# Post-norm attention and mixture of experts on one core: the gate and up products wait by PSUM bank, and the last expert's normalisation is shared out differently

## The reference

```
x = layernorm(x + attn(x))                       # 4 x 2048 tokens of 256 channels, no softmax: causal sigmoid
logits = x @ w_router; top1 of 32 experts; gate = probability of the chosen one
buf[e] = the first C = 320 tokens of expert e
g = buf[e] @ w_gate[e];  u = buf[e] @ w_up[e]     # 320 x 256 by 256 x 256
y = (silu(g) * u) @ w_down[e]
x = layernorm(x + gate * y)                       # (x - mean) / sqrt(var + 1e-5)
```

## Time and profile before

| | |
|---|---|
| time, median of 3 runs | 561.07 us (560.72 to 561.43) |
| profiled execution: its time, its span | 560.36 us, 558.6 us |
| PE, PEld busy in the span | 524.0 us (94%), 458.0 us (82%) |
| DVE, ACT, POOL busy in the span | 407.4 us (73%), 378.3 us (68%), 363.1 us (65%) |
| TensorE clock granted, mean | 0.99 |

### The profile page before, as it was taken

The page is one execution under the profiler, slowest core; times in us unless marked ns, Lnnn a source line. Parts: engine busy times, 40 slices in busy tenths (PEclk is TensorE's granted clock), DMA queues, the critical chain, the costliest instruction groups (busy, mean ns, idle before and its releaser), DMA issues.

```text
span 558.6 us, 12192 instructions
## 1 busy us (share of the span) xinstructions
PE 524.0 (94%) x4028; PEld 458.0 (82%) x4028; DVE 407.4 (73%) x1025; ACT 378.3 (68%) x776; POOL 363.1 (65%) x496
## 2 busy tenths in 40 slices
PE   6999999999999999999999899999999999999970
PEld 5889888898988888888989458888888888888860
DVE  3785868866868856779585637887888888888870
ACT  5886968859778788788686215666666666666641
POOL 4647878787867778786772541566666666666672
PEclk9999999999999999999999999999999999999995
DMA  7994232244332532336901052666666677673200
GB/s 251 375 355 149 76 95 64 93 149 97 115 73 77 165 95 89 61 128 178 341 28 59 21 155 37 201 195 208 201 208 211 191 213 221 207 239 85 60 34 35
DMA packets 91903, 81.54 MB, mean 146 GB/s; under 512 B 31626, under 2 KB 83066, under 8 KB 91840
## 3 DMA queue, kind: packets, MB, share of 16 engines
q1 hardware_dynamic: 84848, 66.39, 40.6%
q0 software_dynamic: 6912, 14.30, 7.3%
q10 hardware_dynamic: 80, 0.07, 0.0%
HBM read 44.33 MB, written 37.90 MB: 147 GB/s over the span
## 4 chain that ended last, share of the span: by engine, by line
PE 75%; DVE 11%; issue 5%; ACT 3%; POOL 3%; DMA 1%; DVEq 0%; POOLq 0%; ACTq 0%; SPq 0%
PE ps L910 11%; PE ps L911 11%; PE ps L912 11%; PE ps L886 10%; PE ps L1063 6%; PE ps L1071 5%; PE ps L1064 5%; DVE v_hl L1265 4%; PE ps L1097 3%; PE ps L1039 3%; PE ps L929 2%; ACT hl_ring L796 2%; DVE hl_ring L1354 2%; PE ps L1089 2%; PE ps L942 1%
## 5 line engine op out<-in xcount | busy, mean ns | idle before, releaser
L910 PE MATMUL ps<-v_hl,hl_ring 128*128 128x256 f32 x544 | 176.0, 323 | 0.4 <-DVE hl_ring L1159 0.3
L911 PE MATMUL ps<-v_hl,hl_ring 128*128 128x256 f32 x544 | 153.4, 282 | 0.0
L912 PE MATMUL ps<-v_hl,hl_ring 128*128 128x256 f32 x544 | 153.1, 281 | 0.0
L910 PEld LDWEIGHTS ps<-v_hl,hl_ring 128*128 128x128 f32 x544 | 103.3, 190 | 15.7 <-issue 1.4
L1159 DVE TENSOR_TENSOR hl_ring<-ps,hl_ring 128x512 fp32r<-128x512 f32 (+3 forms) x160 | 93.2, 601 | 18.0 <-ACT ps L687 14.2
L911 PEld LDWEIGHTS ps<-v_hl,hl_ring 128*128 128x128 f32 x544 | 103.5, 190 | 2.4
L912 PEld LDWEIGHTS ps<-v_hl,hl_ring 128*128 128x128 f32 x544 | 103.2, 190 | 0.0
L685 ACT ACTIVATE hl_ring<-ps 128x512 fp32r<-128x512 f32 (+3 forms) x160 | 85.9, 537 | 23.6 <-PE ps L886 10.5
L886 PE MATMUL ps<-q_t,k_t 128*128 128x512 bf16 (+3 forms) x320 | 85.4, 350 | 2.8 <-ACT k_t L766 1.1
L1063 PE MATMUL ps<-hl_ring,v_hl 128*128 128x320 f32 x256 | 82.0, 332 | 6.2 <-DVE act_r L1373 5.8
L687 ACT ACTIVATE ps<-ps 128x512 f32<-128x512 f32 (+3 forms) x160 | 86.9, 543 | 0.0
(11 more groups left out here) (161 smaller groups left out, 1090.7 us busy)
## 6 DMA issues: line engine op xcount, KB each, us to landing
expert_rows<-xs SPq DMA_DIRECT2D x40, 258.0 KB, 5.6
xs<-expert_rows SPq DMA_DIRECT2D x32, 258.0 KB, 2.9
xall<-in_L_attn_x_dram SPq DMA_DIRECT2D x16, 512.0 KB, 4.4
out_dram<-alone SPq DMA_DIRECT2D x16, 512.0 KB
xall<-in_L_ffn_w_gate_dram SPq DMA_DIRECT2D x32, 256.0 KB, 4.4
xall<-in_L_ffn_w_up_dram SPq DMA_DIRECT2D x32, 256.0 KB, 4.7
xall<-in_L_ffn_w_down_dram SPq DMA_DIRECT2D x32, 256.0 KB, 5.0
xs<-expert_rows SPq DMA_DIRECT2D x31, 64.5 KB
```

Source lines behind the costliest of these rows:

```text
L910: mm(o, ah, v_hl[:, 0, j, :], start=(j == 0 and i % 2 == 0), stop=False, skip_group_check=True)
L911: mm(o, ah, v_hl[:, 1, j, :], start=False, stop=False, skip_group_check=True)
L912: last = mm(o, al, v_hl[:, 0, j, :], start=False, stop=(j == GT * g + i), skip_group_check=True)
```

## The change

1. In `gate_up`, gate's products (u = 0) no longer wait for `hl_ready` or `h_ready` of e-1 but for the silu of e-1 that read gate's bank; up's (u = 1) keep the old wait, which now stands between gate's four matmuls and up's.
2. A constant tile `eps4` (EPS/4) is set by GpSimd at the start, and every wait for the constants counts one more.
3. In the tail ScalarE takes the root of the variances itself, with `eps4` as its bias; VectorE's addition stays, for the Newton step, but ScalarE no longer waits for it.
4. VectorE normalises tile 0 of expert 31 from mean and reciprocal root, ahead of the multiplication by the mean, and GpSimd's store of that tile waits for it (`os_first`). ScalarE keeps tiles 1 and 2.

```diff
@@ block.gpsimd
+            g_.memset(eps4[:, :], EPS / 4).then_inc(consts, 1)
...
                 for t in tiles:
-                    pool.wait_ge(os_ready, tiles_to(e) + t + 1)
+                    if e < E - 1:
+                        pool.wait_ge(os_ready, tiles_to(e) + t + 1)
+                    elif t == 0:
+                        pool.wait_ge(os_first, 1)
+                    else:
+                        pool.wait_ge(os_ready, tiles_to(e) + t)
@@ block.scalar
-                for t in tiles_of(e):
+                for t in tiles_of(e)[e == E - 1:]:
...
             second_norm(RL, 2)
-            act.wait_ge(zq_step, 1)
-            s_.activation(zq[:, 1, :], zq[:, 0, :], ACT.Sqrt).then_inc(root_ready, 1)
+            act.wait_ge(zmv_ready, tiles_to(E))
+            s_.activation(zq[:, 1, :], zmv[:, (E - 1) % 3, :, 1], ACT.Sqrt, bias=eps4[:, 0:1]).then_inc(root_ready, 1)
             second_norm(RL, 3)
@@ block.tensor, gate_up
-                atleast(pe, hl_ready if f == 0 else h_ready, e)
                 lo, hi = turned_cols(e)
                 xh, xl = (x[:, e // 2 % 2, :, lo:hi] for x in (x_h, x_l))
                 for u in range(2):
+                    if u == 0:
+                        atleast(pe, silu_ready, FC * (e - 1) + f + 1 if e > 0 else 0)
+                    else:
+                        atleast(pe, hl_ready if f == 0 else h_ready, e)
                     o = ps[:, 2 + 2 * f + u, 0:CAP]
@@ block.vector, tail
             dve.wait_ge(zq_step, 5)
+            dve.wait_ge(os_out[(E - 1) % 3], stored(E - 4))
+            v_.tensor_scalar(o_s[(E - 1) % 3][:, 0, :], z[:, (E - 1) % 3, 0, :], zmv[:, (E - 1) % 3, 0, 0:1],
+                             zrs[:, (E - 1) % 3, 1, 0:1], ALU.subtract, ALU.mult).then_inc(os_first, 1)
             v_.scalar_tensor_tensor(out=zrs[:, (E - 1) % 3, 2, :], in0=zmv[:, (E - 1) % 3, :, 0], scalar=-1.0,
```

More of the change, by code:

```diff
@@ L105, in bass_postln_attn_moe_kernel @@
         mone = sb("mone", [P, GT], F32)
+        eps4 = sb("eps4", [P, 1], F32)
         bvec = sb("bvec", [P, 2, DC], F32)
@@ L251, in bass_postln_attn_moe_kernel @@
         root_ready = sem("root_ready")
+        os_first = sem("os_first")
         ids_in = [sem(f"ids_in{i}") for i in range(NIDS)]
@@ L263, in atleast @@
                 value = eng.to_reg(value)
-                eng.wait_ge(consts, 10)
+                eng.wait_ge(consts, 11)
             eng.wait_ge(s, value)
@@ L570, in batch @@
                     scatter(n + 2, 0)
-            pool.wait_ge(consts, 10)
+            pool.wait_ge(consts, 11)
             pool.wait_ge(bv_row_ready, 1)
@@ L655, in _ @@
             s_ = nc.scalar
-            act.wait_ge(consts, 10)
+            act.wait_ge(consts, 11)
             s_.activation(spare[:, :], spare[:, :], ACT.Sigmoid).then_inc(table_ready, 1)
@@ L998, in batch @@
                             turn_signs(0, q)
-            pe.wait_ge(consts, 10)
+            pe.wait_ge(consts, 11)
             keep_warm(28, moving=identb[:, :])
@@ L1132, in _ @@
             dve.wait_ge(qksgn_ready, 1)
-            dve.wait_ge(consts, 10)
+            dve.wait_ge(consts, 11)
             def queries(b, q):
```

## The result

The changed kernel takes 556.92 us, the median of 4 runs (556.31 to 558.12), against 561.05 us (560.72 to 561.43, 4 runs) of the kernel before: a ratio of 0.9931 [0.9912, 0.9949], 3.9 us less (of 561.05), give or take one; the two medians lie 4.1 us apart. The profiled execution was the slowest of its four: 558.12 us, its span 556.1 us, where before it was 560.36 and 558.6 us. A few executions in the experiments took far longer than all others (594.75 to 2914.22 us), and ratios and intervals leave them out.

A forecast was written before the change was run, and what follows sets the result against it. TensorE, all but full in the expert stage, was held by a recurring 0.39 us wait at even experts, and GpSimd ended the kernel; 0.30 + 2.38 + 0.34 + 0.18 - 0.03 = 3.17 us gave 557.9 us, range 556.8 to 560.5.

The forecast's parts named there:

- the constants' 0.03 us: At the start, one more memset on GpSimd delays all waits for the constants by 0.03 us.
- expert 1: Gate's first product at expert 1, held by `hl_ready` alone and 0.35 us late, gains 0.30 us.
- 14 periods: Even experts 2 to 28: gate starts 0.34 us earlier, but `down` waiting for `h_ready` leaves 0.17 each, 2.38 us.
- expert 30, up to the variances of 29: In expert 30's turn, the variances of expert 29 come earlier by the full 0.34 us.
- from these variances to GpSimd: GpSimd, which had waited 0.68 us for these variances, follows them with its own row unchanged: 0 us.
- GpSimd's tail: Last stores: GpSimd's spacing of 1.28 us between starts lets the tail gain only 0.18 us (0.0 to 0.2).
- The full wait: Faster rival in the expert loop: VectorE's row doesn't hold `down`, each period gains 0.34 us, 555.5 us; chance 0.10.
- The rival "no change": Expert loop: about four new or moved waits per period, 0.04 us each, eat the 0.17 us; 560.3 us; chance 0.14.
- The rival "slower": The wait between gate's and up's products exposes weight loads in 62 half experts, costing 6.2 us; 564.1 us; chance 0.07.
- 0.36 us would be missing: Tail: without its 0.18 us gain, the old chain would be later against GpSimd and 0.36 us would be missing.
- The 0.85 us from tile to store: Tail: a GpSimd store starts 0.85 us after the tile it waits for, so the first could start at 545.81.
- they gain the 0.34 us there: Expert 29's variances, behind `hidden(30, 0)`, gain 0.34 us; with GpSimd's own row they fix the kernel's end.

The follow-up runs named there:

- the repeat: The unaltered changed kernel run once more beside the kernel before, on a third chip: 557.18 us, ratio 0.9943.
- e5: Changed kernel with `down`'s wait for `h_ready` moved three matmuls later, to its first product with `act_h`: 554.57 us, ratio 0.9888 to the kernel before.
- e6: e5 plus VectorE making the next expert's low weights before its low rows in odd experts' turns: 550.13 us, ratio 0.9821 to the kernel before.
- e12: Kernel before with only VectorE's order altered, low weights before low rows in odd experts' turns: 550.79 us, ratio 0.9826.
- e3: Kernel before with the changed `gate_up`'s waits added and the old wait kept ahead of gate's products: 563.38 us, ratio 1.0035.
- e2: Kernel before with the constant tile, root and last expert's first tile as changed, `gate_up` waiting as before: 559.78 us, ratio 0.9973.
- e11: Kernel before with the changed tail, the constant tile declared last so that no other tile moves: 559.99 us, ratio 0.9993.
- e1: Kernel before with only `gate_up`'s waits changed, tail and constants as before: 557.82 us, ratio 0.9944.
- e8: Kernel before with the constant tile declared last, so no tile moves, plus its memset and count of constants: 560.84 us, ratio 1.0001.
- e4: Kernel before with only the constant tile, its memset and the count of constants, moving later tiles by 32 bytes: 560.48 us, ratio 0.9986.
- e7: Kernel before with the constant tile only declared, no memset or count, later tiles moved by 32 bytes: 560.10 us, ratio 0.9988.
- e10: Kernel before with `gate_up`'s old wait for `hl_ready` or `h_ready` written ahead of the other two: 559.37 us, ratio 0.9981.

## Why the prediction was right, and where it was off

It said 557.9 us (556.8 to 560.5), faster by 3.2 us; it is 556.92, and 557.18 in the repeat. That is inside the whole range by 0.1 us only, and outside the narrower one that the forecast gave for itself, 557.2 to 559.0. By the ratios the gain is 3.9 us, and 3.2 in the repeat. Step by step, for the stretch from the first gate product to the last store (the constants' 0.03 us lie ahead of it):

| step | predicted us | in the trace us |
|---|---|---|
| expert 1 | 0.30 | 0.31 |
| 14 periods | 2.38 (0.17 each) | 2.88 (0.206 each) |
| expert 30, up to the variances of 29 | 0.34 | 0.41 |
| from these variances to GpSimd | 0 | -0.72 |
| GpSimd's tail | 0.18 | 0.18 |
| sum | 3.20 | 3.06 |

- **The bound.** Right: gate comes forward to `wl_ready`, and what is late next is `down`, by `h_ready`. That it is `h_ready`, e5 shows; that `wl_ready` is the other, e6 and e12. The full wait as a rival is out, 12.91 and not 12.78.
- **The step.** I took one delay of 0.14 us from semaphore to product for both cases; it is 0.06 in the changed program, since the last-met wait is now the matmul's own. So gate moved by more than 0.34 us: from the start of L1071's four to gate's first product it was 447.45 - 446.31 = 1.14 us, and is 445.65 - 444.95 = 0.70. And for `down` I took the middle of 0.10 and 0.14; it was 0.10, so it could move by 0.19. The first error is hidden behind `down`; the second is half of the 0.036 us per period by which the term was too small. The other half, 0.02 us, I can't put down to one step.
- **The rival "no change".** The waits that are new cost nothing in the changed kernel. But it was nearer than its reasoning: e3, with the same waits and the old one kept, is slower by 2.0 us. What decided is which wait is met last and where it stands in the program. The order of instructions under "The change" already held the second half of that, and I didn't read it: in its brackets the wait that is on the matmul itself stands last, `wl_ready` both before and after.
- **The rival "slower".** Out: the step over the wait in the middle is 0.14 us.
- **The tail.** The bound by GpSimd's spacing was right, and the 0.18 us is there in the kernel before with the tail alone (e2, e11). In the whole change the number fits by luck. Without the new chain, I said, 0.36 us would be missing; e1 has the old chain and misses nothing (213.90 us against 213.91), because GpSimd is later. So it is GpSimd's lateness that took its wait away, and not parts 3 and 4. The 0.85 us from tile to store, too, was ScalarE's and not VectorE's, whose tile was followed after 0.18.
- **What failed** is the sentence "they gain the 0.34 us there", taken over to the end of the kernel. The variances of expert 29 come (533.78 - 331.90) - (530.76 - 332.48) = 3.60 us earlier, GpSimd only (534.17 - 331.90) - (531.87 - 332.48) = 2.88. GpSimd had waited 0.68 us there, and its own row I had taken as fixed. It isn't: with VectorE's work moved against it, one store in each two experts lasts 2.07 us instead of 1.07. That the sum came so near, 3.06 for 3.20, is luck: two errors of opposite sign, 0.58 and 0.72 us, nearly cancel.
- **Constants and moved tiles.** -0.03 us for the memset can't be seen (e8: 1.0001). The moved tiles, which I had at nothing with up to 2 us in the unseen rest, are worth 0.7 us in the kernel before (e4, e7). They would close the gap from 3.1 to 3.9 us on the first chip, but the repeat doesn't need them. That stays open, and so does why the place of a tile matters.

The whole change is then part 1 (0.9944), perhaps the place of the tiles, and a tail that gains 0.18 us by itself and nothing that the traces show beside part 1. And it isn't the nearest fault: e12, one reordering on VectorE, gives 9.7 us (0.9826 of 560.22).

## What to carry to other kernels

When a wait ends by several semaphores, look first at what makes the last of them late. Here VectorE did work that was ready (weights) behind work that wasn't (rows), and putting that right gave two and a half to three times what splitting the wait gave, and made the split needless. Of several waits ahead of a matmul write first the one that will be met last, so that it lands on the matmul itself, and see in the built program where it went. When an engine off the path moves against another, take its own instructions' durations as open: here the slack at the hand-over was eaten by stores that had become longer.

## What the runs showed of the hardware

- From the end of VectorE's instruction to gate's product that waits for it: 0.06 us with the wait on the matmul (e10, the changed kernel), 0.14 with one semaphore instruction in between (before), 0.25 with two (e3). For `down`, with one in between, it is 0.10 (before, the changed kernel).
- A store of GpSimd that begins inside VectorE's `low_weights` (two inputs in SBUF, 1.48 us) lasts up to 2.40 us (e10; 2.08 in the changed kernel) instead of 0.97 to 1.1, and ends 0.83 to 1.00 us after it. Within 0.05 us behind its start either can win: in e10 the store took 2.39 us nine times, and five times 1.07 us, with `low_weights` 0.07 us longer.
- Beside a store, small instructions of VectorE were longer too, and ended with the store or 0.13 us behind it: 0.38 instead of 0.17 us, 0.65 instead of 0.41 (the changed kernel).
- A tile that is declared and not used lowered the time by 0.12% [0.04%, 0.21%] (e7), nearly all of it ahead of the expert stage.
- A first product that waits costs about 0.1 us more than its wait: the next product follows 0.22 us (before) or 0.25 us later (the changed kernel), not 0.15.
